# Attention of two layers: scores of two entries together, value products between two groups of transposes

## The reference

```python
x = x + _L0_xattn_ref(_layernorm(x), ctx, Wq, Wk, Wv, Wo, bo)        # 16 heads of 64
x = x + _L0_ffn_ref(_layernorm(x), w1, conv_w, conv_b, w2)           # 256 -> 1024 -> 256, ternary weights
x = x + _L1_xattn_ref(_layernorm(x), ctx, Wq, Wk, Wv, Wo, q_norm_w, k_norm_w)   # 16 heads of 16
x = x + _L1_ffn_ref(_layernorm(x), w1, b1, w2, b2)                   # quantised over the whole tensor
```

## Time and profile before

| | |
|---|---|
| median of 3 runs | 2503.68 us (2501.91 to 2503.96) |
| the profiled execution | 2504.27 us |
| its span | 2502.5 us |
| mean granted clock of TensorE | 0.987 |
| busy, us: TensorE, its weight loads, VectorE, ScalarE, GpSimd | 2395.5, 1789.6, 1716.0, 1594.5, 1595.0 |
| score matmuls (line 399), two groups | 230.5 and 227.8 us |
| transposes (line 409), two groups | 238.4 and 238.0 us |
| row maxima (line 984) | 479.7 us |

### The profile page before, as it was taken

One profiled execution on the slowest core, in us unless ns is written; L12 is line 12 of the kernel. 1 busy time (PEld: TensorE's weight loads), 2 busy tenths in 40 slices (PEclk: granted clock), 3 DMA queues, 4 the chain that ended last, 5 costly groups with the idle time before them and its releaser, 6 DMA issues.

```text
span 2502.5 us, 59414 instructions
## 1 busy us (share of the span) xinstructions
PE 2395.5 (96%) x18926; PEld 1789.6 (72%) x18926; DVE 1716.0 (69%) x4475; ACT 1594.5 (64%) x4337; POOL 1595.0 (64%) x1846
## 2 busy tenths in 40 slices
PE   7999999999999999999999999999999999999567
PEld 5777777777777777777777777777777777777336
DVE  6666666676666667766666676666667666666777
ACT  4666666766666667666666766666676666666446
POOL 2666676666667766666776666667666666776506
PEclk9999999999999999999999999999999999999689
DMA  4000000000000000000000000000000000000202
GB/s 154 27 10 10 10 8 10 2 10 10 10 10 10 8 4 8 10 10 10 10 8 7 4 10 10 10 10 8 10 2 10 10 10 10 10 2 3 53 8 60
DMA packets 34524, 37.02 MB, mean 15 GB/s; under 512 B 2804, under 2 KB 32964, under 8 KB 34500
## 3 DMA queue, kind: packets, MB, share of 16 engines
q1 hardware_dynamic: 34500, 36.71, 4.9%
HBM read 29.36 MB, written 7.34 MB: 15 GB/s over the span
## 4 chain that ended last, share of the span: by engine, by line
PE 75%; DVE 10%; issue 5%; ACT 5%; POOL 4%; DMA 0%; ACTq 0%; DVEq 0%; SPq 0%; POOLq 0%
PE pt L409 16%; PE ps L330 16%; PE ps L399 14%; PE pa L421 7%; PE pa L456 5%; PE ps L383 5%; DVE z L1130 4%; PE pa L436 4%; POOL prob L1403 2%; ACT prob L755 2%; DVE nmx L984 1%; POOL qrs L1446 1%; PE ps L649 1%; PE pt L553 1%; PE ps L449 1%
## 5 line engine op out<-in xcount | busy, mean ns | idle before, releaser
L984 DVE TENSOR_REDUCE nmx<-ps 112x2 f32<-112x750 f32 x512 | 479.7, 937 | 199.8 <-PE ps L399 199.7
L1403 POOL TENSOR_TENSOR prob<-prob,rinv 112x375 f32<-112x375 f32 x512 | 405.7, 814 | 222.5 <-DVE rinv L1000 216.5
L1403 POOL TENSOR_TENSOR f1w_room<-f1w_room,rinv 112x375 f32<-112x375 f32 x512 | 404.6, 815 | 63.3 <-DVE rinv L1000 54.8
L716 ACT ACTIVATE room<-ps 128x375 f32<-128x375 f32 (+2 forms) x480 | 228.0, 488 | 290.5 <-PE ps L330 290.5
L975 DVE COPY probT<-pt 125x336 f32<-125x336 f32 x512 | 254.1, 496 | 116.2 <-PE pt L409 116.2
L716 ACT ACTIVATE probT<-pt 125x336 f32<-125x336 f32 x512 | 231.4, 452 | 118.0 <-PE pt L409 114.9
L409 PEld LDWEIGHTS pt<-ident,prob 112*125 112x125 f32 x1536 | 190.9, 189 | 129.6 <-issue 69.5
L409 PEld LDWEIGHTS pt<-ident,f1w_room 112*125 112x125 f32 x1536 | 196.7, 187 | 119.0 <-issue 54.4
L1426 POOL TENSOR_TENSOR krs<-krs,nhalf 125x48 f32<-125x48 f32 x32 | 257.0, 8031 | 0.0
L399 PE MATMUL ps<-kT,q 64*112 64x375 f32 x1024 | 230.5, 528 | 17.0 <-ACT f1w_room L755 14.6
L409 PE MATMUL pt<-ident,f1w_room 112*125 112x112 f32 x1536 | 238.0, 286 | 2.6 <-DVE probT L975 1.3
(11 more groups left out here) (261 smaller groups left out, 5164.6 us busy)
## 6 DMA issues: line engine op xcount, KB each, us to landing
ctok<-in_ctx SPq DMA_DIRECT2D x32, 375.0 KB
xin<-in_x SPq DMA_DIRECT2D x32, 112.0 KB, 2.0
x_rows<-x SPq DMA_DIRECT2D x32, 112.0 KB, 1.9
out<-probT SPq DMA_DIRECT2D x8, 448.0 KB, 3.2
room<-x_rows SPq DMA_DIRECT2D x1, 2576.0 KB, 14.2
stage<-in_f1w SPq DMA_DIRECT2D x2, 1024.0 KB, 5.2
stage<-in_wk SPq DMA_DIRECT2D x1, 1024.0 KB, 8.5
stage<-in_wv SPq DMA_DIRECT2D x1, 1024.0 KB, 10.7
```

Of the source, the lines that this page charges most:

```text
L716: return act.activation(dst, src, ACT.Copy)
L984: top = dve.tensor_reduce(nmx[:, g:g + 2], ps[0:T, 2 * (i % 2):2 * (i % 2) + 2, 0:S], AX_X, ALU.max, negate=True)
L1403: pool.tensor_tensor(prob(i, n), prob(i, n), rinv[:, g:g + 1].to_broadcast([T, S]), ALU.mult).then_inc(s["normed"], 1)
```

## The change

**Middle attention, TensorE.** The order is by two iterations. With i even: scores of i+2, scores of i+3, transposes of i-1, value products of i-4 and i-3, and then (i+1) the transposes of i. Layer 0 leads by four entries (`LEAD = 4`), so that entries 0 to 3 and 12 to 15 are layer 0's and 4 to 11 layer 1's. **ScalarE** does `exps(i + 2)` first and then `turned(i - 1)`. **VectorE** takes the maxima of both new entries before the sums and the copy.

**Entry.** The query transposes and their copies move from `rest` into the middle attention: on TensorE behind the scores of entry 2, on ScalarE behind the copy of entry 2's transposes (iteration 3), on VectorE behind the maxima of entry 2. GpSimd normalises entries 0 and 1 before the first root and then alternates roots and entries.

**Projections.** Key piece 4 is split: three of its matmuls go before the transposes of `xq`, three behind the diagonal product. Value piece 2 is split: two before the transposes of `th`, four behind `x0_transpose`.

**End.** Additions and stores are done by halves of a chunk, with a semaphore for each half (`o3_low`, `o3_high`); from the second chunk on `round_rows` comes before the first maximum.

```diff
         AHEAD = 2
+        LEAD = 4
...
-            if i < AHEAD:
+            if i < LEAD:
                 return 0, i
-            return (1, i - AHEAD) if i < AHEAD + PAIRS else (0, i - PAIRS)
+            return (1, i - LEAD) if i < LEAD + PAIRS else (0, i - PAIRS)
...
-                    if i + AHEAD < count:
+                    if i + AHEAD < count and (part != MIDDLE or i % 2 == 0):
                         scores(i + AHEAD, part, b)
                     if part == MIDDLE and i == 0:
+                        query_turn(b)
                         pe.wait_ge(s["q1_sq"], b + 1)
                         v0_proj(b + 1, [5])
+                    if part == MIDDLE and i % 2 == 0 and i + AHEAD + 1 < count:
+                        scores(i + AHEAD + 1, part, b)
...
                     if i >= 1:
                         turn(i - 1, part, b)
...
+                        if i >= 4 and i % 2 == 0:
+                            values(i - 4, part, b)
...
                 if not last_batch:
-                    k0_proj(b + 1, range(0, 5), True)
+                    k0_proj(b + 1, range(0, 4), True)
+                    pe.wait_ge(s["k0_sb"], b * IC + (IC + 1))
+                    k0_terms(4, 0, 3)
...
+                if not last_batch:
+                    k0_terms(4, 3).then_inc(s["k0_ready"], 1)
...
+                    v0_terms(2, 0, 2)
...
-                    v0_proj(b + 1, [2])
+                    v0_terms(2, 2).then_inc(s["v0_ready"], 1)
...
                 for i in range(count):
-                    if part == MIDDLE and i == AHEAD + PAIRS + 2:
+                    if part == MIDDLE and i + AHEAD < count:
+                        exps(i + AHEAD, part, b)
+                        if i == 0:
+                            v0_copy(b + 1, [5])
+                    if i >= 1:
+                        turned(i - 1, part, b)
+                    if part == MIDDLE and i == 3:
+                        query_copies(b)
+                    if part == MIDDLE and i == LEAD + PAIRS + 2:
                         o1_copy(part, b)
...
-                    if i >= 1:
-                        turned(i - 1, part, b)
-                    if i + AHEAD < count:
+                    if part != MIDDLE and i + AHEAD < count:
                         exps(i + AHEAD, part, b)
...
-                    if i + AHEAD < count:
+                    if i + AHEAD < count and (part != MIDDLE or i % 2 == 0):
                         row_max(i + AHEAD, part, b)
...
+                    if part == MIDDLE and i % 2 == 0 and i + AHEAD + 1 < count:
+                        row_max(i + AHEAD + 1, part, b)
...
             for c in range(NCH):
+                if 0 < c < NCH - 1:
+                    next_rows(c)
                 largest(c, 0)
                 largest(c, 1)
...
+                for n in range(2):
+                    half = slice(2 * n, 2 * n + 2)
+                    pool.wait_ge(s["o3_sum"], c * 2 + (n + 1))
```

More of the change, by code:

```diff
@@ L317, in _, with exact3 @@
             with sp.Fori(0, NCH) as c:
-                sp.wait_ge(s["o3_sum"], c + 2)
-                sp.dma_start(out_rows[c], outc).then_inc(s["o3_out"], 16)
-            sp.wait_ge(s["o3_out"], 16 * NCH + 16)
+                for n in range(2):
+                    sp.wait_ge(s["o3_sum"], c * 2 + (n + 3))
+                    sp.dma_start(out_rows[c][:, 2 * n:2 * n + 2, :], outc[:, 2 * n:2 * n + 2, :])\
+                        .then_inc(s[("o3_low", "o3_high")[n]], 16)
+            sp.wait_ge(s["o3_low"], 16 * NCH + 16)
+            sp.wait_ge(s["o3_high"], 16 * NCH + 16)
         @block.tensor
         def _(pe):
[L325 to L330, removed]
+            TERMS = [(l, r, c) for l, r in ((1, 0), (0, 1), (0, 0)) for c in range(DC)]
+            def exact3(dst, left, right, first=0, end=len(TERMS)):
+                for n, (l, r, c) in list(enumerate(TERMS))[first:end]:
+                    last = pe.matmul(dst, left(l, c), right(r, c), start=(n == 0), stop=(n == len(TERMS) - 1))
                 return last
@@ L458, in wo0_product, with values, query_turn @@
                     last.then_inc(s["wo_ready"], 1)
+            def values(i, part, b):
+                if pair_of(i, part)[0] == 0:
+                    values0(i, part, b)
+                    values0(i + 1, part, b)
+                else:
+                    values1(i, part, b)
+            def query_turn(b):
+                pe.wait_ge(s["q1_rope"], b + 1)
+                for c in range(DC):
+                    last = pe.transpose((pt[:, 0], pa[:, 1])[c][:, 0:T], q1b[:, c * P:(c + 1) * P], ident[0:T, 0:T])
+                last.then_inc(s["q1T_ready"], 1)
             def attention(part, b):
@@ L572, in rest @@
                     v0_proj(b + 1, [4])
-                pe.wait_ge(s["q1_rope"], b + 1)
-                for c in range(DC):
-                    last = pe.transpose((pt[:, 0], pa[:, 1])[c][:, 0:T], q1b[:, c * P:(c + 1) * P], ident[0:T, 0:T])
-                last.then_inc(s["q1T_ready"], 1)
-                if not last_batch:
                     pe.wait_ge(s["v0_sb"], b * 6 + 10)
@@ L788, in attention, with query_copies @@
                     o1_copy(part, b)
+            def query_copies(b):
+                act.wait_ge(s["q1T_ready"], b + 1)
+                for m in range(4):
+                    ins = act.activation(q1[:, 1, m, :], pa[:, 1, 0:T], ACT.Copy, scale=mask1[:, m:m + 1])
+                ins.then_inc(s["q1_sb_act"], 1)
             def o1_copy(part, b):
-                act.wait_ge(s["pv"], at(PAIRS + (AHEAD if part == MIDDLE else 0), part, b))
+                act.wait_ge(s["pv"], at(PAIRS + (LEAD if part == MIDDLE else 0), part, b))
                 copy(oT1[:], pa[:, 1, 0:DC * T].rearrange("p (j t) -> p j t", j=DC)).then_inc(s["o_sb"], 1)
@@ L1449, in rest @@
                 part = CLOSING if last_batch else MIDDLE
-                for n in range(2):
-                    query_root(n)
-                attention(part, b, 1 if part == MIDDLE else 0, 2)
-                query_root(2)
-                attention(part, b, 2, 3)
-                query_root(3)
-                attention(part, b, 3, G if part == MIDDLE else PAIRS)
+                if part == MIDDLE:
+                    for n in range(4):
+                        query_root(n)
+                        attention(part, b, n + 2, n + 3)
+                    attention(part, b, 6, G)
+                else:
+                    query_root(0)
+                    query_root(1)
+                    attention(part, b, 0, 2)
+                    query_root(2)
+                    attention(part, b, 2, 3)
+                    query_root(3)
+                    attention(part, b, 3, PAIRS)
             pool.wait_ge(s["zeros_ready"], 1)
```

104 lines of the change are left out of this document (58 added, 46 removed), and 1 row of the table names.

## The result

The changed kernel takes **2642.2 us** (median of 4 runs, 2640.9 to 2643.04) against 2503.82 us (2501.91 to 2504.75) for the kernel before, now with a fourth run: a ratio of 1.0553, interval 1.0535 to 1.0572. The forecast was 2633, range 2580 to 2690. The profiled execution has a span of 2641.2 us, 138.7 more than 2502.5.

A forecast was written before the change was run, and what follows sets the result against it. TensorE, busy 96% of the span, was taken to set the time. Rounds +5.53, entry -0.73 and split -0.48 gave +4.32 us a batch, +133.9 in 31 batches; with -4.5 at the end, 2633, range 2580 to 2690.

The forecast's parts named there:

- The chain as the gate: Middle attention: even transposes wait for scores, maximum, exponentials and ScalarE's copy, 4.39 us; 5.22 a layer-1 round; chance 0.80.
- Layer-0 rounds: Middle attention, two entries with layer-0 scores: the same chain without scaling, 3.61 us, with the transposes 4.44 a round.
- a sign of being wrong: Rounds under 4.15, even transposes waiting for GpSimd's normalisation or the odd copy, or granted clock below 1.00 in the loop.
- The end of a batch: Last round: entry 13's transposes wait for a copy behind entry 15's exponentials, 5.17 after entry 14's scores; projection at 6.72.
- Entry and split: Start of the middle attention and split key and value projections: 0.73 and 0.48 us less a batch.
- The 0.46 fills it and eats the 0.2: Split projections: a moved 0.46 us value product fills a 0.32 wait for VectorE and cancels the key split's 0.2.
- The end: End of the kernel: earlier rounding in the maxima pass saves 1.5 us, additions and stores by halves 3.
- The clock: Rival: TensorE's granted clock falls in one round of each batch, costing 43 us, 2676 in all; chance 0.08.
- Faster: Rival: even transposes find ScalarE's copy already done, the gate does not bind, 97 us saved, 2403; chance 0.10.
- half covered: Rival: about half of the chain is covered by something unseen, cost and gain cancel, near 2504; chance 0.02.

The follow-up runs named there:

- Experiment 1: The kernel before, with ScalarE in the middle attention doing the exponentials of entry i+2 ahead of the copy of entry i-1's transposes, nothing paired: 2902.22 us.
- experiment 3: The changed kernel with ScalarE's order in the middle attention made copy, both entries' exponentials, copy: 2562.44 us.
- experiment 2: The changed kernel with ScalarE's old order in the middle attention, copy of entry i-1's transposes first, then exponentials of entry i+2: 2631.04 us.
- experiment 5: The kernel before with the two split projections of the change alone: 2483.82 us.

## Why the prediction was right

- **The chain as the gate: right.** Predicted 5.22 a round with layer-1 scores; measured 5.22 in three rounds and 5.35 in the first (1025.86 to 1031.21), where the second scores wait 0.75 for the exponentials of entry 3 and are not joined. The links came out at 0.93, 1.59, 1.30, 0.59 and 0.81 against 0.93, 1.57, 1.30, 0.59 and 0.83. Experiment 1 shows the loop made by ScalarE's order alone, experiment 3 that another order frees 80 us of the 192 that the middle attention loses. What I had not seen, and experiment 2 showed, is that the old order would not have saved the change: a second loop, through the two score slots, takes 5.37 with layer 0's value products and leaves the period at 76.03 against 76.46.
- **Layer-0 rounds: right, one link short.** 4.44 predicted, 4.50 measured (1046.87 to 1051.37). From the maximum to the exponentials it took 1.06 instead of 0.98. The profile's rows name GpSimd at the even transposes here, which the prediction had as a sign of being wrong; the entries counted above show that it was the copy all the same.
- **The end of a batch.** S(14) to T(13) 5.14 and to the projection 6.66, against 5.17 and 6.72. S(4) to the projection 32.17 against 32.04.
- **Entry and split: both undersized.** The entry gave 0.93 (9.10 to 8.17) instead of 0.73, the split 0.68 a batch instead of 0.48 (21.2 in 31), just beyond its stated bound of 0.66. "The 0.46 fills it and eats the 0.2; the transposes start where they did" was wrong: in experiment 5 the transposes of `th` start 8.20 behind those of `xq` instead of 7.76, and the two fillings add. Where the entry's other 0.2 came from I did not follow. Together with 5.66 for the rounds that is +4.05 a batch; 4.09 was measured, 4.32 predicted.
- **The end: mis-sized.** 4.5 taken. By the traces the maxima pass, from its first to its last maximum, gave 3.6 instead of 1.5 (40.97 to 37.4; a chunk went from 5.39 to 4.59). From there to the end it was 5.5 instead of 3 (74.19 to 68.72), beyond the stated "0 to -5": I read only the last chunk's wait of 0.93 for a store and not the 1.78 for VectorE in the chunks ahead of it. These 9 us are the same in the changed kernel and in the end alone. That the one shows only 6.9 from the last batch on, and the other's runs 11.4, comes at least in part from stretches that the end does not touch: between the last transposes of `xq` and the first maximum the profiled executions of all the kernels took anything from 61.4 to 65.7, the changed one the longest.
- **The clock: a rival that came true in part, and in part luck.** I gave it 0.08 as one case against the others, at 43 us for every batch, and named a granted clock below 1.00 in the loop as a sign of being wrong. It came on top of the gate, in 11 of 31 batches, at 19.1 us, a term that the sum had at nothing. Without it the time would have been about 2623, 10 below the forecast, since the gains were undersized (some 12 for entry and split, less 4 that the rounds took more, and 2 to 7 for the end). The forecast of 2633 came within 9 of 2642 because these errors partly cancel.
- **Faster, and half covered:** neither. In the batch shown TensorE arrived at the even transposes before the copy in every round.

## What to carry to other kernels

Before two steps are swapped on one engine, write out the loop that closes through the single buffer: who must read it before it is written again, and what stands before that reader on its engine. A saving on the busy engine (0.19 us for joined scores) is real and still worth nothing where the order that brings it puts a chain of 4.4 us between two of that engine's steps. And price the parts of a change one by one: here three parts of four gain 55 us together, and the fourth hides it.

## What the runs showed of the chip

- The granted clock fell to 0.50 behind the same two waits (0.75 and 1.17 to 1.19; in the first batch 1.43) in 11 of the first 30 batches of one execution and not in the others, which have the same matmuls. Over a whole batch the mean is 0.978 in batches longer by 1.2 to 1.4 us, 0.957 in those longer by 2.2 to 2.3, and 1.000 in the others. In experiment 1 every batch had some of it (0.92 to 0.98). In experiment 2 batches of 76.0 at 1.000 and of 77.6 at 0.978 took turns but for a few (two at 0.957 took 78.9), with the same instructions.
- Four matmuls that compute nothing, filling 0.93 of a wait of 1.17, kept the clock at 1.00 in all but the last batch and made the kernel 18 us faster.
- What a profile's row names as the end of a wait can be another entry's event that fell at the same time: the first half of GpSimd's normalisation of entry 11 ended at 1050.55, 0.01 before T(10), which waited for ScalarE's copy. Counting the instructions of each line through the program tells them apart.
